# Turned scores in two products on operands laid out by transfers, a ring for x, and new orders and banks

## The chip, the cores and the metric

The kernel runs on one core of one Trainium2 chip. Five engines work side by side, each with its own instruction stream: TensorE (PE) multiplies matrices into eight PSUM banks, VectorE (DVE), ScalarE (ACT) and GpSimd (POOL) do elementwise work, and SyncE (SP) issues the transfers (DMA) between device memory and on-chip memory. They wait for each other through semaphores. The metric is the device time of one execution in microseconds.

## What is computed

A batch of 64 images with 256 positions and 320 channels passes two cross-attention layers, each with 20 heads of 16 channels and a context of 77 tokens of 512 channels.

```
layer 0:  q = x Wq^T,  k = text Wk^T,  v = text Wv^T          (77 text tokens)
          out = softmax(q k^T / 4) v  per head;  x = out Wo^T + bo + x
layer 1:  73 text tokens and 4 image tokens
          q = x W_q;  text_out = softmax(q k^T / 4) v;  probs_t = the same softmax
          qsem = l2norm(probs_t text);  sem = qsem . l2norm(image tokens)
          fused = q k_ip^T / 4 + 0.5 sem;  probs_ip = softmax(fused) * spatial_mask
          out = (text_out + probs_ip v_ip) W_out + b_out + x
```

## The kernel before

**Two stages.** `keys_and_values` multiplies the whole context with the key, value and image weights, in eight chunks of eight batches, and stores keys, values and the Gram matrix of the text (used for the norm of qsem) to device memory (`k_dram`, `v_dram`, `g_dram`). `attention` then runs over the 64 batches, both layers.

**Precision by parts.** Inputs are float32. A product that must be accurate is made from float16 parts: a high part and a low part, the rest. For q k^T three products are summed: high keys with high q, high keys with low q, low keys with high q.

**Layout.** 320 channels are three chunks of 128, the last one with its 64 channels doubled. A group of 32 partitions holds two heads of 16 channels. Keys are stored twice, once with zeros for the even head of a group and once with zeros for the odd one (`half_keys` with its `e`, scaled by `pscale`), so that a multiply over 32 partitions sees one head alone.

**Scores twice.** `scores` (L979) multiplies high parts only, with positions on the output partitions, and VectorE takes the negated maxima over the tokens (`maxima`, L1202). The maxima are turned by a transpose (`turn_max`) and copied to `mt`. `turned_scores` (L1009) makes the scores again with the tokens on the output partitions: three products, and a fourth that adds the maxima, for which a table of ones (`sel`) is the stationary operand. Four multiplies, one on each group of 32 rows, stand side by side. The exponential (`exponentials`, L1143) follows on ScalarE. In layer 1 ScalarE then halves it to float16 (`halves`), GpSimd takes the rest, TensorE multiplies with the Gram matrix (`gram_products`, L1053), VectorE weights the result (`weighted`, L1230), and `square_norms` sums it.

**What sets the order.** Every engine runs a cyclic list of steps, `ORDER` (L126). A step such as `1u2/3` means layer 1, gram product of unit 2, of the batch three behind the newest; `q` is the query projection, `s` scores, `m` turn of maxima, `t` turned scores, `a` attention sums, `n` norms, `i` and `p` the image tokens' scores and output, `o` the output projection, `y0` to `y19` the steps of the image softmax, `w` the weighting, `ql` the low part of q, `d` inverses, `g` and `at`/`al` the attended rows, `r` the residual. On SP, `k`, `v`, `x` load, `ds`, `sh`, `rw`, `rl` move denominators, move numerators, store and spread inverses. `USES` (L144) gives for each of the eight banks the cycle of its users; `Turns.wait` (L188) makes a step wait until the previous user of each of its banks has been read. Steps on one engine never overtake each other, and SP issues all transfers in the order of its list.

**Buffers.** x of layer 0 and of layer 1 have two buffers each, the residual with bias (`res`) and the output (`outt`) have two of their own, the spread inverses `rb` have one for each layer. The even head's numerators are moved to their partitions by four transfers (L894).

## Time and profile before

| | us |
|---|---|
| three timed runs | 2445.96, 2448.13, 2452.12 |
| median | 2448.13 |
| span of the profiled execution | 2447.7 |
| TensorE busy | 2259.4 (92%) |
| ScalarE busy | 1728.4 (71%) |
| VectorE busy | 1702.0 (70%) |
| GpSimd busy | 1592.2 (65%) |
| DMA queue q1, share of 16 engines | 44.7% |

The page gives no time of the profiled execution besides its span, so the time to compare with is 2447.7 us. Up to about 319 us the first stage runs, then the loop over batches. Busy time of TensorE is the time in which at least one multiply is in flight; a row that groups multiplies which run side by side adds their overlapping times only partly. A timeline row merges neighbours of one form; its first number is the start, the second the time to the end of the last. "PEclk" is the granted clock as a share of full speed.

### The profile page before, as it was taken

Reading aid. Unit: us, or ns where it says so; the run is one execution under the profiler, and the core shown is the slowest. Engines: PE = TensorE matmul, PEld = TensorE weight load, DVE = VectorE, ACT = ScalarE, POOL = GpSimd, SP = SyncE. Lnnn points to the kernel's source line nnn. Section 1 sums busy time; section 2 is a strip of 40 time slices with the busy share of each in tenths; the row PEclk is TensorE's granted clock in tenths of the full one; section 3 lists DMA queues with packets and bytes.
Section 4 is the critical chain, followed back from the end, with each engine's and each line's share of the span. In section 5 each row is a group of like instructions: output and inputs, shape, how many; then the busy total and the mean of one; then the engine's idle time right before and its main releaser. Section 6 shows DMA issues by size and latency. Waiting matters only on the chain.

```text
span 2447.7 us, 90636 instructions
## 1 busy us (share of the span) xinstructions
PE 2259.4 (92%) x35896; PEld 1464.0 (60%) x35896; DVE 1702.0 (70%) x2860; ACT 1728.4 (71%) x2604; POOL 1592.2 (65%) x1056
## 2 busy tenths in 40 slices
PE   8999958999999999999999999999999999999984
PEld 6777735655566665666556555666566655555642
DVE  5543425777777777777777777777777777777763
ACT  4332327778878777787787787877877787787861
POOL 4121135777777777777777776777777777777762
PEclk9999969999999999999999999999999999999996
DMA  9968622444444444444344444444444444444421
GB/s 275 281 209 235 194 89 70 117 115 117 118 114 114 118 115 116 118 115 117 111 118 119 115 114 114 113 118 115 115 118 118 114 113 115 114 119 116 119 80 56
DMA packets 338318, 310.92 MB, mean 127 GB/s; under 512 B 180224, under 2 KB 281856, under 8 KB 337920
## 3 DMA queue, kind: packets, MB, share of 16 engines
q1 hardware_dynamic: 337920, 305.36, 44.7%
q8 instruction: 281, 4.60, 0.8%
q14 instruction: 117, 0.96, 0.1%
HBM read 164.66 MB, written 105.98 MB: 111 GB/s over the span
## 4 chain that ended last, share of the span: by engine, by line
PE 46%; DVE 23%; ACT 7%; issue 5%; DMA 3%; SPq 2%; DVEq 0%; POOL 0%; ACTq 0%; POOLq 0%
PE psum L1065 12%; PE psum L966 10%; PE psum L1049 8%; PE psum L1028 7%; DVE q_low L1220 4%; ACT q_high L1136 4%; DVE mneg L1213 3%; PE psum L969 3%; ACT ef L1154 3%; DVE e L1235 3%; DVE sq L1254 2%; DVE outt L1313 2%; PE psum L1032 2%; PE psum L991 2%; DVE x1b L1313 1%
## 5 line engine op out<-in xcount | busy, mean ns | idle before, releaser
L1381 POOL TENSOR_TENSOR e<-ef,eh 73x1024 f32<-73x1024 f32 x320 | 681.1, 2129 | 300.4 <-ACT eh L1169 257.0
L1154 ACT ACTIVATE ef<-psum 73x1024 f32<-73x1024 f32 (+1 forms) x640 | 628.0, 1011 | 90.9 <-PE psum L1032 87.4
L1235 DVE TENSOR_TENSOR e<-psum,e 73x1024 f32<-73x1024 f32 x320 | 386.7, 1209 | 135.6 <-PE psum L1065 135.3
L1213 DVE TENSOR_REDUCE mneg<-psum 128x8 f16<-128x616 f32 (+3 forms) x512 | 446.9, 923 | 34.9 <-PE psum L991 34.1
L1065 PE MATMUL psum<-eh,gram 128*73 128x512 f16 x1280 | 340.9, 390 | 45.2 <-ACT ef L1154 16.0
L1049 PE MATMUL psum<-ef,values 128*32 128x256 f32 x5120 | 351.4, 389 | 7.7 <-DVE pip L1295 5.9
L1028 PE MATMUL psum<-q_high,keys 32*73 32x256 f16 (+2 forms) x6144 | 324.7, 258 | 34.0 <-DVE mneg L1213 21.6
L1169 ACT ACTIVATE eh<-ef 73x1024 f16<-73x1024 f32 x320 | 337.0, 1053 | 16.2 <-ACT ef L1154 0.4
L1220 DVE SCALAR_TENSOR_TENSOR q_low<-psum,q_high 128x640 f16<-128x640 f32 x128 | 105.5, 824 | 262.3 <-ACT q_high L1136 262.3
L1028 PEld LDWEIGHTS psum<-q_high,keys 32*73 32x73 f16 (+1 forms) x6144 | 186.9, 110 | 144.5 <-issue 68.7
L1162 ACT ACTIVATE ust<-psum 128x512 f32<-128x512 f32 x384 | 223.4, 594 | 67.1 <-PE psum L1049 60.5
L1348 POOL TENSOR_TENSOR al<-ust,ah 128x768 f16<-128x768 f32 x128 | 210.6, 1645 | 86.9 <-ACT ah L1192 86.6
L1343 POOL TENSOR_TENSOR ust<-ust,rb 128x768 f32<-128x768 f32 x128 | 231.8, 1811 | 17.9 <-DMA rb<-r_dram 17.8
L1065 PEld LDWEIGHTS psum<-eh,gram 128*73 128x73 f16 x1280 | 121.9, 115 | 173.0 <-ACT ef L1154 47.0
L1049 PEld LDWEIGHTS psum<-ef,values 128*32 128x32 f32 x5120 | 128.9, 109 | 136.3 <-issue 30.4
L966 PE MATMUL psum<-ah,wo 128*128 128x256 f16 x1280 | 194.7, 275 | 13.2 <-POOL al L1348 13.2
L1032 PE MATMUL psum<-mt,sel 32*73 32x256 f16 (+3 forms) x3072 | 205.2, 251 | 0.0
L1028 PE MATMUL psum<-q_low,keys 32*73 32x256 f16 (+3 forms) x3072 | 205.2, 251 | 0.0
L1077 PE MATMUL psum<-e,pick 128*32 128x256 f32 x2560 | 165.8, 386 | 2.6 <-DVE e L1235 2.6
L966 PE MATMUL psum<-xh,wq 128*128 128x256 f16 x1024 | 155.8, 275 | 5.7 <-PEq L230 4.1
L1192 ACT ACTIVATE ah<-ust 128x768 f16<-128x768 f32 x128 | 107.5, 840 | 66.1 <-POOL ust L1343 56.2
L966 PEld LDWEIGHTS psum<-ah,wo 128*128 128x128 f16 x1280 | 119.2, 98 | 45.3 <-DVE e L1235 17.4
(180 smaller groups left out, 4530.3 us busy)
## 6 DMA issues: line engine op xcount, KB each, us to landing
rb<-r_dram SPq DMA_DIRECT2D x128, 384.0 KB, 4.1
keys<-k_dram SPq DMA_DIRECT2D x128, 231.0 KB, 3.6
values<-v_dram SPq DMA_DIRECT2D x128, 192.5 KB
ust<-ust SPq DMA_DIRECT2D x512, 48.0 KB, 2.5
v_dram<-vst SPq DMA_DIRECT2D x64, 320.0 KB
out<-outt SPq DMA_DIRECT2D x64, 320.0 KB, 2.2
k_dram<-kst SPq DMA_DIRECT2D x32, 616.0 KB, 4.8
x<-in_x SPq DMA_DIRECT2D x32, 384.0 KB, 3.7
```

The source lines that it names most:

```text
L966: mm = pe.matmul(o[:, c * S:(c + 1) * S], a, data[:, k, :], **at_ends)
L1028: pe.matmul(o, keys(l, low, c)[rows, e, 0:n], q[rows, cols], start=(low == 0 and q is qh[l]), stop=False)
L1032: mm = pe.matmul(o, sel[rows, k, 0:n], mt[l][rows, lead:lead + many], start=False, stop=True)
L1049: mm = pe.matmul(row(l, f"a{c}")[j * SLOT:(j + 1) * SLOT, r * S:(r + 1) * S], va[l][:, h, :], e, start=True, stop=True)
L1065: mm = pe.matmul(banks(l, f"u{k}", 2)[0:n, r, :], gm[:, b.parity(), half, :], e, start=(half == 0), stop=(half == 1))
L1154: act.activation(ef[l][0:m, unit_heads(n), :].rearrange("t h s -> t (h s)"), src, ACT.Exp, scale=SM).then_inc(s_exp[l], 1)
L1162: act.activation(ust[l][:, b.parity(), :, c, :], src, ACT.Copy).then_inc(s_u[l], 1)
L1169: act.activation(eh[0:m, unit_heads(k), :], ef[1][0:m, unit_heads(k), :], ACT.Copy, scale=0.5)\
L1213: dve.tensor_reduce(dst, o, AX_X, ALU.max, negate=True).then_inc(s_max[l], 1)
L1235: dve.tensor_tensor(rest, banks(l, f"u{k}", 2)[0:m, :, :], rest, ALU.mult).then_inc(s_wr, 1)
L1343: pool.tensor_tensor(at(l, b), at(l, b), rb[l][:], ALU.mult).then_inc(s_at[l], 1)
L1381: pool.tensor_tensor(e2[0:m, k, :, :], ef[1][0:m, unit_heads(k), :], eh[0:m, unit_heads(k), :], ALU.subtract).then_inc(s_e2, 1)
```

## The change

- `turned_scores` has two products instead of four. The heads' channels are interleaved, so that in a group of 32 partitions even rows belong to one head and odd rows to the other. For one head, `tq` holds on the rows of that head's partner copies of its own q rows: on every pair of rows the same source row. The first product multiplies it with `paired_keys` (high keys on one row of a pair, low keys on the other), the second multiplies `marked_keys` (high keys on one row, ones at marked places on the other) with the low part of q and the maxima. Transfers build all this: `load_key_tiles` issues three for a set of keys, `turn_queries` (`tq`) two, `place_maxima` (`tm`) two.
- In the first stage keys are copied once, in high and low part, and stored in halves of their former size, with smaller rows.
- x lives in a ring of six buffers through both layers; bias, layer output and final output are written in place. `res` and `outt` are gone. `rb` is one buffer for both layers.
- Numerators are moved by one transfer instead of four, inverses stored once instead of twice and spread by two transfers.
- `ORDER` and `USES` are new; waits for banks come from the whole order, and a step that uses two banks can wait for the second one later (`only`).

```diff
-DEN, SEM4 = D, D + 1
+DEN = 1
+KC = CW * T
+QW = PW
+TW = QW + CW * S
+RING = 6
...
 ORDER = {
     "pe": """
-        1u2/3 1a1/3 0t1/1 1q/2 0t2/1 0a0/1 1s0/2 0a1/1 1s1/2 0a2/1 1a2/3 1i/2 1u3/3 1m/2 1u4/3 1t0/2 0q/0
-        1n0/3 1n1/3 1p/4 0s0/0 1n2/3 1n3/3 1n4/3 0s1/0 1t1/2 1a0/2 1u0/2 1t2/2 1u1/2 1o/4 0m/0 0o/1 0t0/0""",
+        0m/1 1u0/3 0o/2 1u1/3 0t0/1 1a1/3 1u2/3 0t1/1 1q/2 0t2/1 0a0/1 0a1/1 1s0/2 0a2/1 1n0/3 1a2/3 1s1/2 0q/0 1u3/3
+        1m/2 1u4/3 1n1/3 1p/4 1n2/3 1n3/3 1n4/3 1i/2 1t0/2 0s0/0 0s1/0 1t1/2 1o/4 1y/3 1t2/2 1a0/2""",
     "act": """
-        1a1/3 1f/4 0t2/1 0t3/1 1q/2 0t4/1 1h4/3 0a0/1 0a1/1 0a2/1 1a2/3 1i/2 1m/2 0r/0 1t0/2 1h0/2 0q/0
-        1t1/2 1h1/2 1n/3 1g/4 1t2/2 1t3/2 1a0/2 0g/1 1t4/2 1h2/2 0m/0 1r/2 1h3/2 0t0/0 0t1/0""",
+        1t4/3 1h1/3 0m/1 1h2/3 1a0/3 1h3/3 0t0/1 0t1/1 1a1/3 1f/4 0t2/1 0t3/1 1q/2 0t4/1 0a0/1 0a1/1 0a2/1 1h4/3 1a2/3
+        0r/0 1r/2 1m/2 0q/0 1g/4 1n/3 1i/2 1t0/2 1t1/2 1h0/2 1t2/2 1t3/2 0g/1""",
     "dve": """
-        1y10/4 1y11/4 0o/2 1y12/4 1y13/4 1y14/4 1w2/3 1y15/4 1y16/4 1y17/4 1y18/4 1y19/4 1ql/2 1s0/2 1s1/2
-        1s2/2 1s3/2 1w3/3 0d/1 1w4/3 0ql/0 1p/4 0s0/0 0s1/0 0s2/0 1d/3 0s3/0 1w0/2 1w1/2 1y0/3 1y1/3 1y2/3
-        1y3/3 1o/4 1y4/3 1y5/3 1y6/3 1y7/3 1y8/3 1y9/3""",
+        1y0/4 1y1/4 1y2/4 1y3/4 1y4/4 1y5/4 1w0/3 1y6/4 1y7/4 1y8/4 1y9/4 1y10/4 0o/2 1y11/4 1w1/3 1y12/4 1y13/4
+        1y14/4 1y15/4 1w2/3 1y16/4 1y17/4 1y18/4 1y19/4 1ql/2 1s0/2 1s1/2 1s2/2 1s3/2 0d/1 1w3/3 1w4/3 1p/4 0ql/0
+        0s0/0 0s1/0 0s2/0 0s3/0 1d/3 1o/4""",
     "pool": """
-        1xh/2 1xl/2 1b3/3 1b4/3 0xh/0 1vb/4 0xl/0 1kb/1 1c/2 1at/4 1b0/2 1b1/2 1al/4 0at/1 0al/1 1b2/2""",
+        0al/2 1b1/3 1b2/3 1xh/2 1xl/2 1b3/3 1at/4 0xh/0 0xl/0 1kb/2 1b4/3 1c/2 1vb/4 1al/4 0at/1 1b0/2""",
     "sp": """
-        1ss/3 1sl/3 1rl/4 1sh/4 0x/0 1vi/4 1ps/4 0ds/1 1v/2 1pl/4 1ds/3 0k/0 0rw/1 0sh/1 0rl/1 1g/2 1c/1
-        0v/0 1ns/3 1rw/3 1nl/3 1k/1 1d/3 1st/4""",
+        0x/0 1rw/4 1vi/4 0tm/1 0v/1 1rl/4 1c/2 1st/5 1sh/4 1k/2 1sl/3 1ps/4 0k/0 1tq/2 1pl/4 0ds/1 1v/2 0rw/1 1tm/2
+        0rl/1 1ds/3 0sh/1 1ns/3 1d/3 0tq/0 1nl/3 1g/1 1ss/2""",
...
 USES = [
-    "0t3/1 0a0/1 0a2/1 1u3/3 0q/0 0s0/0 0s2/0 1u1/2 0m/0 0t1/0",
-    "0t3/1 0t4/1 1s1/2 1u3/3 0q/0 0s0/0 0s2/0 1a0/2 1u1/2 0t1/0",
-    "1a1/3 0t4/1 1s1/2 1i/2 1u4/3 1n/3 1t2/2 1u0/2 1o/4",
-    "0t2/1 0t4/1 1s3/2 1u4/3 1p/4 1t2/2 1u0/2 1o/4 0t0/0",
-    "0t2/1 0t4/1 1s3/2 1t0/2 1p/4 0s3/0 1t4/2 0t0/0",
-    "1u2/3 1q/2 1s0/2 1s2/2 1m/2 1t0/2 1p/4 0s3/0 1t4/2 0o/1",
-    "1u2/3 1q/2 1s0/2 1s2/2 1t1/2 0s1/0 1t3/2 1t4/2 0o/1",
-    "0a1/1 1a2/3 1t1/2 0s1/0 1t3/2 1t4/2 1y/3",
+    "1u1 1u2 0t4 1n 0s0 0s3 1t4",
+    "1u1 1u2 0t4 1s1 0q 0s0 0s3 1t4",
+    "1u0 0t0 0t3 0t4 1s1 0q 0s1 1t3 1t4",
+    "1u0 0t0 0t3 0t4 1s0 1s3 1u3 1p 1i 0s1 1t3 1t4",
+    "1a1 1q 1s0 1s3 1u3 1p 1t1 1t2 1a0",
+    "0o 0t1 0t2 1q 0a2 1s2 1m 1p 1t1 1t2",
+    "0m 0o 0t1 0t2 0a0 1s2 1u4 1t0 0s2 1o",
+    "0a1 1a2 1u4 1t0 0s2 1o 1y",
...
+def load_key_tiles(sp, ka, ks, src, loaded):
+
+    both_parts = src.rearrange("a x (r f) n -> (a r) x (f n)", f=2)
+    sp.dma_start(ka[:].rearrange("p f n -> p (f n)"), both_parts).then_inc(loaded, 16)
+    for e in (0, 1):
+        high = src[:, 0, 1 - e:P:2, :].rearrange("a r n -> (a r) n")
+        sp.dma_start(ks[1 - e:P:2, e, :, :], high.unsqueeze(1).to_broadcast([HALF, 2, KC])).then_inc(loaded, 16)
+
+
+KLOADS = 3
...
+                dst = [k_dram[l][bass.DynSlice(batch, CB), :, :, :].rearrange("b x p n -> x p b n") for l in both]
+                for l in both:
+                    results_of("k", l, 1)
+                    for x in (0, 1):
+                        keys = kst[l][:, x, :, :, :].rearrange("p b c t -> p b (c t)")
+                        sp.dma_start(dst[l][x, :, :, 0:2 * T], keys).then_inc(s_kstored, 16)
+                results_of("kt", 0, 1)
+                for l in both:
+                    for x in (0, 1):
                         for copy in (0, 1):
-                            tail = ktail[l * HALF:(l + 1) * HALF, half, :, :, :, :].rearrange("p b h e t -> p b (h e t)")
-                            sp.dma_start(dst[l][copy * HALF:(copy + 1) * HALF, :, 8 * T:], tail)\
-                              .then_inc(s_kstored[half], 16)
+                            sp.dma_start(dst[l][x, copy * HALF:(copy + 1) * HALF, :, 2 * T:],
+                                         ktail[l * HALF:(l + 1) * HALF, x, :, :]).then_inc(s_kstored, 16)
...
-                        for e in (0, 1):
-                            ins = act.activation(half_keys(kind, l, c, half, 0, e), by_batch(psum[:, r, 0:HT], T), ACT.Copy,
-                                                 scale=pscale[:, e:e + 1])
-                        ins.then_inc(s_khigh, 1)
+                        act.activation(half_keys(kind, l, c, half, 0), by_batch(psum[:, r, 0:HT], T), ACT.Copy,
+                                       scale=1 / WS).then_inc(s_khigh, 1)
...
+        xr = [early.xin] + [sb(f"x_ring{n}", [P, CW, S]) for n in range(1, RING)]
         xh = [early.xh, sb("xh1", [P, CW, S], F16)]
         xl = [early.xl, sb("xl1", [P, CW, S], F16)]
-        res = [sb(f"res{l}", [P, 2, (CW * S, PW)[l]]) for l in both]
-        qh = [sb(f"q_high{l}", [P, PW], F16) for l in both]
-        ql = [sb(f"q_low{l}", [P, PW], F16) for l in both]
-        ke = [early.ke, sb("keys1", [P, 2 * CW * 2 * T], F16)]
+        qq = [sb(f"q_parts{l}", [P, 2, QW], F16) for l in both]
+        qh, ql = [[qq[l][:, n, :] for l in both] for n in (0, 1)]
+        tq = [sb(f"turned{l}", [P, 2, TW], F16) for l in both]
+        ka = [early.ka, sb("keys1", [P, 2, KC], F16)]
+        ks = early.ks
...
+        def plain_keys(l, c):
+            return ks[l][:, :, 0, c * T:(c + 1) * T]
+
+        def paired_keys(l, e, c):
+            return ka[l][:, 1 - e, c * T:(c + 1) * T]
+
+        def marked_keys(l, e, c):
+            return ks[l][:, e, 1, c * T:(c + 1) * T]
...
+            def turn_queries(l, b, n):
+
+                b.reached(sp, f_t[l], CW, 0)
+                b.reached(sp, s_ql[l], 1, 1)
+                for e in (0, 1):
+                    rows = qq[l][1 - e:P:2, :, :].rearrange("p h n -> p (h n)")
+                    sp.dma_start(tq[l][:, e, 0:2 * QW], rows.unsqueeze(1).to_broadcast([HALF, 2, 2 * QW]))\
+                      .then_inc(s_tq[l], 16)
+
+            def place_maxima(l, b, n):
+
+                b.reached(sp, s_tq[l], 32, 32)
+                b.reached(sp, s_mt[l], 1, 1)
+                for e in (0, 1):
+                    dst = tq[l][e:P:2, e, QW:].rearrange("p (c s) -> p c s", c=CW)
+                    sp.dma_start(dst, mt[l][e:P:2, :].unsqueeze(1).to_broadcast([HALF, CW, S])).then_inc(s_tm[l], 16)
...
-                for j in range(NJ):
-                    sp.dma_start(ust[l][j * SLOT + D:(j + 1) * SLOT, b.parity(), 0, :, :],
-                                 ust[l][j * SLOT:j * SLOT + D, b.parity(), 1, :, :]).then_inc(s_num[l], 16)
+                sp.dma_start(ust[l][1:P:2, b.parity(), 0, :, :], ust[l][0:P:2, b.parity(), 1, :, :]).then_inc(s_num[l], 16)
 
             def store_inverses(l, b, n):
                 b.reached(sp, s_rd[l], 1, 1)
-                for copy in (0, 1):
-                    dst = r_dram[l][b.parity()][:, copy, :].rearrange("h (q i) -> h q i", i=QS)
-                    sp.dma_start(dst, rd[l][:, b.parity(), :]).then_inc(s_rw[l], 16)
+                dst = r_dram[l][b.parity()].rearrange("j r (q i) -> (j r) q i", i=QS)
+                sp.dma_start(dst, rd[l][:, b.parity(), :]).then_inc(s_rw[l], 16)
 
             def spread_inverses(l, b, n):
                 b.reached(sp, s_at[l], 1, 0)
-                b.reached(sp, s_rw[l], 32, 32)
-                src = r_dram[l][b.parity()].rearrange("h k n -> (h k) n").unsqueeze(1).to_broadcast([2 * HC, D // 2, CW * S])
-                sp.dma_start(rb[l][:].rearrange("p c s -> p (c s)"), src).then_inc(s_rb[l], 16)
+                before = spread_before(l, b)
+                if before is not None:
+                    sp.wait_ge(s_at[before[0]], before[1] + 1)
+                b.reached(sp, s_rw[l], 16, 16)
+                for r in (0, 1):
+                    src = r_dram[l][b.parity()][:, r, :].unsqueeze(1).to_broadcast([NJ, D, CW * S])
+                    sp.dma_start(rb[r:P:2, :, :].rearrange("p c s -> p (c s)"), src).then_inc(s_rb[l], 16)
...
-                    b.reached(pe, s_ql[l], 1, 1)
-                    b.reached(pe, s_mt[l], 1, 1)
+                    b.reached(pe, s_tm[l], 32, 32)
                 for e in range(2):
                     if c < 2:
                         tiles = [(slice(j * SLOT, (j + 1) * SLOT),
                                   banks(l, uses[j // 2], 2)[0:n, j % 2, e * S:(e + 1) * S]) for j in range(NJ)]
-                        cols, many = slice(c * S, (c + 1) * S), S
+                        cols = slice(c * S, (c + 1) * S)
                     else:
                         tiles = [(slice(j * SLOT, (j + 1) * SLOT), banks(l, "t4", 4)[0:n, j, e * TS:(e + 1) * TS])
                                  for j in range(NJ)]
-                        cols, many = slice(2 * S, PW), TS
-                    for low, q in ((0, qh[l]), (0, ql[l]), (1, qh[l])):
-                        for rows, o in tiles:
-                            pe.matmul(o, keys(l, low, c)[rows, e, 0:n], q[rows, cols], start=(low == 0 and q is qh[l]),
-                                      stop=False)
+                        cols = slice(2 * S, PW)
                     for rows, o in tiles:
-                        k, lead = (2 * c + e, 0) if c < 2 else (2 * c, e * many)
-                        mm = pe.matmul(o, sel[rows, k, 0:n], mt[l][rows, lead:lead + many], start=False, stop=True)
+                        pe.matmul(o, paired_keys(l, e, c)[rows, 0:n], tq[l][rows, e, cols], start=True, stop=False)
+                    for rows, o in tiles:
+                        mm = pe.matmul(o, marked_keys(l, e, c)[rows, 0:n], tq[l][rows, e, QW:2 * QW][:, cols], start=False,
+                                       stop=True)
...
                 b.reached(pe, s_eh, UNITS, k + 1)
                 for r in range(2):
+                    if r:
+                        wait_free(pe, l, b, f"u{k}", only=1)
...
             def residual(l, b, n):
-                b.reached(act, (s_x, s_xo[0])[l], (16, 1)[l], (16, 1)[l])
-                b.reached(act, s_xo[l], 1, -1)
+                b.reached(act, s_xl[l], 1, 1)
+                data = x_of(b)
                 for c in range(CW if l == 0 else 2):
-                    ins = act.activation(res[l][:, b.parity(), c * S:(c + 1) * S], xin[l][b.parity()][:, c, :], ACT.Identity,
-                                         bias=bias_sb[l][:, c:c + 1])
+                    ins = act.activation(data[:, c, :], data[:, c, :], ACT.Identity, bias=bias_sb[l][:, c:c + 1])
...
             def output(l, b, n):
                 b.reached(dve, s_rs[l], 1, 1)
-                if l == 0:
-                    b.reached(dve, s_xl[1], 1, -1)
-                    b.reached(dve, s_rs[1], 1, -1)
-                else:
-                    b.reached(dve, s_store, 16, -16)
                 b.reached(dve, f_o[l], 1, 1)
-                dst, n = (xin[1][b.parity()][:].rearrange("p c s -> p (c s)"), CW * S) if l == 0 else (outt[:, b.parity(), :], PW)
-                dve.scalar_tensor_tensor(dst, row(l, "o", 2)[:, 0:n], 1 / WS, res[l][:, b.parity(), :], ALU.mult,
+                data, n = x_of(b)[:].rearrange("p c s -> p (c s)"), (CW * S, PW)[l]
+                dve.scalar_tensor_tensor(data[:, 0:n], row(l, "o", 2)[:, 0:n], 1 / WS, data[:, 0:n], ALU.mult,
```

## Rows read from the trace of the kernel before

**Rows 1.** busy by stage: start:end, length, PE, PEld, DVE, ACT, POOL, PEclk, DMA, GB/s
```profile
180.00:240.00 60.00, 60.00 (x642) 47.35 (x641) 21.96 (x52) 17.31 (x41) 9.15 (x2) 1.00 0.85 242
...
330.00:360.00 30.00, 12.67 (x195) 8.01 (x196) 5.42 (x7) 9.94 (x15) 11.05 (x7) 0.61 0.22 59
...
420.00:1100.00 680.00, 646.56 (x11019) 408.30 (x11021) 519.41 (x865) 543.36 (x796) 502.16 (x342) 1.00 0.42 115
...
1254.92:1286.54 31.62, 30.18 (x519) 19.01 (x515) 24.25 (x40) 25.29 (x38) 23.52 (x17) 1.00 0.43 116
```

**Rows 2.** page, costliest groups: line, engine, operation, tiles, count, busy us, mean ns
```profile
L1235 DVE TENSOR_TENSOR e<-psum,e 73x1024 f32<-73x1024 f32 x320 | 386.7, 1209 | 135.6 <-PE psum L1065 135.3
...
L1028 PE MATMUL psum<-q_high,keys 32*73 32x256 f16 (+2 forms) x6144 | 324.7, 258 | 34.0 <-DVE mneg L1213 21.6
...
L1032 PE MATMUL psum<-mt,sel 32*73 32x256 f16 (+3 forms) x3072 | 205.2, 251 | 0.0
L1028 PE MATMUL psum<-q_low,keys 32*73 32x256 f16 (+3 forms) x3072 | 205.2, 251 | 0.0
```

**Rows 3.** timeline of TensorE, turned scores: start, time to the end, line, forms
```profile
1275.35 0.25 PE L1028 MATMUL psum<-q_high,keys 32*73 32x128 f16 x4
...
1282.07 0.31 PE L1028 MATMUL psum<-q_high,keys 32*77 32x256 f16 x4
...
1282.86 0.28 PE L1032 MATMUL psum<-mt,sel 32*77 32x256 f16 x4
```

**Rows 4.** timeline of TensorE, starts of long steps and of what follows them
```profile
1265.31 0.61 PE L966 MATMUL psum<-xh,wq 128*128 128x256 f16 x4
...
1267.73 1.07 PE L1077 MATMUL psum<-e,pick 128*32 128x256 f32 x16
...
1275.93 1.06 PE L1065 MATMUL psum<-eh,gram 128*73 128x512 f16 x4
1276.82 0.60 PE L966 MATMUL psum<-ah,wo 128*128 128x256 f16 x4
...
1279.23 0.29 PE L1005 MATMUL psum<-ident,mneg 128*128 128x128 f16 x2
```

**Rows 5.** timeline of VectorE, ScalarE and TensorE behind an output and turned scores
```profile
1282.53 0.96 DVE L1313 SCALAR_TENSOR_TENSOR x1b<-psum,res 128x768 f32<-128x768 f32 x1
...
1283.34 1.91 ACT L1154 ACTIVATE ef<-psum 77x1024 f32<-77x1024 f32 x2
...
1283.55 1.06 PE L1065 MATMUL psum<-eh,gram 128*73 128x512 f16 x4 [0.41 <-DVE x1b L1313]
```

**Rows 6.** timeline of ScalarE, copies behind the norms
```profile
1271.51 0.38 ACT L1175 ACTIVATE nst<-psum 128x256 f32<-128x256 f32 x1 [0.81 <-PE psum L1077]
1271.79 0.84 ACT L1192 ACTIVATE ah<-ust 128x768 f16<-128x768 f32 x1
```

**Rows 7.** timeline of TensorE and VectorE, two score steps and the maxima
```profile
1259.25 0.31 PE L991 MATMUL psum<-keys,q_high 32*128 32x146 f16 x8 [0.26 <-DVE q_low L1220]
...
1260.51 0.31 PE L991 MATMUL psum<-keys,q_high 32*128 32x146 f16 x8
...
1259.68 3.39 DVE L1213 TENSOR_REDUCE mneg<-psum 128x8 f16<-128x584 f32 x4 [0.49 <-PE psum L991]
```

**Rows 8.** transfers, 1000 to 1640 us: packets, MB, share; issues, KB, us to landing
```profile
q1 hardware_dynamic: 82241, 72.38, 41.3%
...
rb<-r_dram SPq DMA_DIRECT2D x41, 384.0 KB, 4.2
...
ust<-ust SPq DMA_DIRECT2D x164, 48.0 KB, 2.5
```

**Rows 9.** timeline of SyncE, issues of transfers in one period
```profile
1265.40 1.42 SPq L901 DMA_DIRECT2D r_dram<-rd  x2
...
1269.86 0.56 SPq L907 DMA_DIRECT2D rb<-r_dram  x1
```

**Rows 10.** transfers, 0 to 300 us: packets, MB, share of 16 engines
```profile
q1 hardware_dynamic: 72750, 71.98, 81.2%
```

297 lines of the change are left out of this document (151 added, 146 removed).

## The prediction

> **What bounds the kernel now.** Read the stage table first, then the costliest lines, then a period's timeline. In the projection stage TensorE is busy without a gap (60.00 of 60.00 us) at a granted clock of 1.00; in the attention loop it is busy 646.56 of 680 us, ScalarE 543, VectorE 519, GpSimd 502 [rows 1]. One period, from one layer-1 query projection to the next, takes 31.62 us; over many, 31.7. TensorE ends the period, but the other three have 24 to 25 us of work in it. A change that shortens TensorE by more than a few us meets them, and all four feed each other through the banks.
>
> The turned scores look like the largest item: 12,288 multiplies on L1028 and L1032, whose groups' busy times sum to 735 us [rows 2], 11.5 us a period. That sum is a trap. Four multiplies on four row groups run together, and the next four follow 0.11 us later while the first are still in flight: eight such groups start between 1282.07 and 1282.86, so a whole step takes 0.88 us and not eight times 0.28; the short step, from 1275.35 to the next step at 1275.93, takes half of it, 0.47, and a gap [rows 3, 4]. A period has four long steps and two short ones: 4.5 us of TensorE's time, not 11.5.
>
> **The change on TensorE.** Each step goes from eight groups to four: a long one 0.88 to 0.45 us, a short one 0.47 to 0.25. Saved: 4 x 0.43 + 2 x 0.22 = 2.2 us a period, 64 x 2.2 = 138 us, if nothing else ends there. By steps, from the start of one to the start of the next, what stays: five gram steps of 0.89 (1275.93 to 1276.82), two query projections of 2.42, the output projections of 2.41 and, with the turn of the maxima in front, 2.84 (1279.23 to 1282.07) [rows 3, 4], attention sums, norms, scores and the small ones together about 10 us; with the new turned scores 27.3 us. Before: 29.4, so 2.3 us of each 31.7 were waits.
>
> **What the new order waits for.** I walked the new orders and bank lists through one period, time 0 at the layer-0 turn of the maxima, with durations of the rows, and looked for each step at the last reader of its banks.
> - 1u0 follows the exponential of 1t4 in the same bank: start 0.45 instead of 0.1.
> - 0o ends at 4.1. 0t1 has its banks, so VectorE's output add must be through; from the output's last issue to TensorE's next start that took 1.48 us (1282.07 to 1283.55, the add 0.96) [rows 3, 5]: 0t0 at 5.55, a wait of 0.55.
> - 0t1 takes the banks of 0t0's two exponentials, 1.91 us for the pair [rows 5]: 8.45, a wait of 0.5. Then 1q, 0t2 and two sums, 1s0 at 13.7, 0q from 15.75, 1u3 until 19.1.
> - VectorE weights 1u3 and 1u4 (1.21 us each [rows 2]) and adds the image part (0.96, as the add of the same size in rows 5): 22.6. ScalarE then copies 0.84, 0.38 and about 0.37 [rows 6]: 24.25. 0s0 needs the bank of the last: 24.4.
> - 0s1 comes straight behind 0s0, and its second use has 0s0's banks. Start of scores to start of the maxima 0.43, and to the next scores 1.26 [rows 7]. Before, three norm steps filled this; now nothing does: 0s1 at 25.65, a wait of 1.0.
> - 1t1 waits for two exponentials (26.55, a wait of 0.6), 1o for the third maximum of layer 0 (27.5, 0.4). 1o 2.41, 1t2 0.4, 1a0 0.9: the next turn at 31.25.
> Waits with two small ones (1t0 and 0s0, 0.45 together): 3.9 us. The period is 27.3 + 3.9 = 31.2, I take 31.25: of 2.2 us saved, 1.6 go back into waits, most of them in the 4 us around 0s0, where ScalarE's own chain would end only some 0.6 us earlier. So 64 x 0.45 = 29 us are gained.
>
> **The transfers.** Added per layer and batch: two of 320 KB that lay out the interleaved rows (256 packets of 2560 B) and two that place the maxima (384 packets of 512 B); key loads go from 1 to 3 (128 packets to 384, same bytes). Away: three of four numerator moves and one inverse store. Per period (640 us hold 20.2) the bytes go from 3.6 to 5.3 MB, the packets from 4070 to 5670 [rows 8]. A packet now takes 51 ns (0.413 x 16 x 640 us over 82,241) [rows 8]; at that, 290 engine-us of 16 x 31.25 = 500, 58%; by bytes 310, 62%. Not a bound as a sum.
>
> A wait is added in front of the turned scores: maxima copied, then two issues, then landing. No row shows this transfer. The nearest small one, 48 KB, lands in 2.5 us, the 384 KB one in 4.2 [rows 8]; an issue takes 0.6 to 0.7 [rows 9]. From below 0.7 + 2.5 = 3.2 us, from above 1.4 + 4.2 = 5.6. The order leaves 3.8 us on layer 0 (mt 1.75, 0t0 5.55) and 3.3 on layer 1 (20.35 to 23.65). I take 3.2, the row nearest in size: just hidden. At the upper end both are late and a period would be up to 4.1 us longer. Queued behind the waiting placement on SP are the values, the inverses' spread and the layer-1 stores; GpSimd's multiply by the inverses waits for these, with 2 us to spare in my walk. The query layout is issued about 5 us ahead of its use and hidden.
>
> SP itself: 35 issues a period become 41. At 0.56 to 0.71 us each [rows 9] that is 23 to 29 us of 31.25, with landings to wait for in between (inverses, norms, probabilities).
>
> The single buffer for the inverses couples the layers; its reader is done 10 us before the next load. The ring for x and the residual in place take two buffers and no work away. Nothing on these, from -0.1 to +0.2 us a period: the waits they replace (load of x, output store) end no step in the rows.
>
> **Stage one.** Keys are copied once instead of twice on ScalarE and VectorE. TensorE fills that stage alone [rows 1], so this is worth nothing. Key stores halve in bytes but double in packets (4096 to 8192 a chunk, of 308 and 154 B). Mean cost of a packet now: 0.812 x 16 x 300 us / 72,750 = 54 ns [rows 10]. Per chunk of 36 us the DMA time changes by -7 us (by bytes) to +14 (by packets). With 29 us used (81%) it becomes 22 to 43 us. I take about +3, since in the loop 60% of the packets are under 512 B and the mean is still 51 ns [rows 8]: hidden behind TensorE, 0 us.
>
> **Filling and draining.** In the first and last periods one batch's chain sets the time (TensorE 12.67 of 30 us busy, clock 0.61 [rows 1]). The placement of the maxima stands in it bare: about 2.5 us more for each layer at one end, +5 us (bounds 0 to +20).
>
> **Sum.** The profiled execution's span is 2447.7, the median of the runs 2448.1; they agree within 0.5, and I go from the latter. 2448 - 29 + 5 = 2424.
>
> **Rivals.**
> A, TensorE alone decides: its waits stay at 2.3 us a period although the work shrinks. 2448 - 138 + 5 = 2315. For it: TensorE is the busiest by 5 us. Against: the bank reuse at 0s1, 0t0 and 0t1 is forced by the list. Half of it (waits 3.1) gives 2366.
> B, slower: the placement of maxima is late. SP comes to it late behind the x load, the inverse store and the wait for norms (in my walk it gets there about when the maxima do), or the transfer queues behind 655 KB of query rows. It decides from 0.45 us a period on; with 0.5 us on each layer, 1.0 in all, the period is 32.25 and the time 2448 + 35 + 5 = 2488. For it: SP has 2 to 8 us left, the slack on layer 1 is 0.1. Against: DMA is idle 40% of the time.
> C, slower in stage one: small packets cost as much as large ones, DMA needs 43 us for 36 of TensorE, 7 us x 7 chunks = +49: 2473. Against: the loop's 51 ns. The Trainium skill (DMA: Bandwidth & Descriptors, Specifications) says that transfers below 512 B fall short of the line rate since a read-modify-write is done; by that rule both new store sizes pay, and C is what it would give. The rows do not separate packet sizes, so it is not settled by them.
> D, the clock: TensorE's busy share falls from 0.95 to 0.90. [...] Left at 2%.
>
> **Chances.** My forecast (2395 to 2445) 0.45; A or its half 0.20; B 0.21; C 0.08; the rest (D, a walk wrong by more, other causes) 0.06. A walk of this kind errs by some 0.6 us a period, 38 us. The range 2350 to 2478 leaves out A in full and the bad end of B. About 0.3% (7 us) can be told from no change: faster 0.59, within 0.14, slower 0.27.
>
> **What would show it.** Steps of turned scores of 0.45 us. A gap of about 1 us on TensorE between the first and second score steps of layer 0, released by the maxima; gaps of 0.5 before 0t0 (output add) and 0t1 (exponentials). If the first is absent, A gains. TensorE waiting for a transfer ahead of the turned scores is B. Stage one ending later than 319 us, with DMA above 95%, is C. A loop period outside 30.6 to 31.9 us would make the forecast wrong.

## The result, and the profile after

The changed kernel takes 2704.44 us, median of four runs (2696.22 to 2715.94); the kernel before took 2449.61 us on the same chip (2445.96 to 2452.12). The ratio is 1.1046, 95% interval 1.1015 to 1.1077: 255 us slower, where 2424 us was forecast and the range ended at 2478. The profiled execution took 2707.64 us, its span is 2705.8 us.

The stage table of the changed kernel, with the columns of [rows 1]; the first two windows lie in the projection stage, the third where the first batch fills the loop:

```profile
120.00:180.00 60.00, 60.00 (x558) 46.65 (x556) 12.31 (x31) 8.54 (x22) 15.16 (x4) 1.00 1.18 134
180.00:240.00 60.00, 60.00 (x643) 47.40 (x641) 15.36 (x41) 12.55 (x34) 12.29 (x3) 1.00 0.94 202
330.00:360.00 30.00, 9.13 (x114) 5.47 (x118) 8.65 (x6) 7.27 (x10) 17.32 (x10) 0.56 0.36 125
420.00:1100.00 680.00, 567.50 (x7952) 343.53 (x7950) 467.64 (x754) 466.41 (x702) 444.53 (x304) 0.94 0.49 147
```

Against [rows 1] every engine does less in the loop: TensorE 567.50 of 680 us instead of 646.56, ScalarE 466 instead of 543. No engine has become the bound. What rises is the transfers' share, 0.42 to 0.49, which still looks far from full. The granted clock falls from 1.00 to 0.94. A period, from one store of the image probabilities (L978) to the next, runs from 1209.92 to 1246.38 us: 36.5 us instead of 31.62; 18 periods in 640 us make 35.6 on average against 31.7. The two profiled spans differ by 258 us. 18 of these lie in the projection stage, which ends at 337.6 instead of 319.7 us; the other 240 are the longer periods.

The chain of waits of the page names who sets the end, first by engine and then by line, each with its share of the span:

```profile
DMA 29%; PE 19%; SPq 14%; issue 9%; POOL 9%; DVE 4%; ACT 3%; POOLq 0%; ACTq 0%; DVEq 0%
DMA rb<-r_dram 13%; PE psum L1014 10%; DMA den<-ust 5%; DMA n_dram<-nst 5%; POOL ust L1391 4%; SPq L888 3%; DMA r_dram<-rd 2%; PE psum L1113 2%; SPq L953 2%; POOL al L1396 2%; ACT ef L1207 2%; PE psum L1075 2%; SPq L245 2%; SPq L879 2%; PE psum L1017 2%
```

The first is a transfer, the spread of the inverses. The same chain inside one period (start, length, what):

```profile
1214.58 4.37 DMA den<-ust
...
1219.04 0.56 DVE rd L1281
1219.61 0.31 SPq L943
...
1220.02 0.66 SPq L888
1220.72 0.64 SPq L888
...
1221.47 0.57 SPq L953
1222.08 6.61 DMA rb<-r_dram
1228.73 0.82 issue
1229.58 1.82 POOL ust L1391
...
1233.44 1.64 POOL al L1396
...
1235.22 4.33 PE psum L1014 x24
```

Denominators land, VectorE inverts them, the inverses are stored, two placements of maxima are issued in between, then the spread takes 6.61 us to land. GpSimd waits for it, and TensorE for GpSimd. The output projection at the end takes 4.33 us for 24 multiplies, since the granted clock is 0.50 in its first 3 us. Four windows of the changed kernel show that: an output at full clock; a gap of TensorE, behind which come one gram step at full clock and another wait of 0.85 us; the slow output; and what follows.

```profile
1227.40:1230.10 2.70, 2.68 (x48) 2.22 (x48) 1.62 (x3) 1.74 (x2) 0.52 (x1) 1.00 0.50 171
1231.60:1233.20 1.60, 0.00 (x0) 0.00 (x0) 0.00 (x0) 1.60 (x3) 1.60 (x1) 1.00 0.33 96
1235.20:1238.20 3.00, 2.98 (x15) 2.13 (x16) 2.79 (x9) 1.65 (x3) 3.00 (x2) 0.50 0.55 151
1239.00:1242.00 3.00, 2.70 (x41) 1.51 (x39) 2.35 (x4) 0.55 (x1) 1.36 (x3) 1.00 0.69 202
```

A granted clock of 0.50 is 1.2 GHz. So a transfer that is late by 4 us can cost more than 4 us: from its start to the next step the slow output takes 4.16 us, the one at full clock 2.42. This is no exception. Between 420 and 2300 us, in some 53 periods, the clock records of the changed kernel have 50 stretches at 0.50, 188 us together; those of the kernel before have one. The landings, from 1000 to 1640 us (issues, KB each, median us to landing), beside [rows 8]:

```profile
q1 hardware_dynamic: 102930, 94.13, 49.2%
...
turned<-q_parts SPq DMA_DIRECT2D x72, 320.0 KB, 3.9
rb<-r_dram SPq DMA_DIRECT2D x72, 192.0 KB
...
turned<-mt SPq DMA_DIRECT2D x72, 96.0 KB, 2.1
...
ust<-ust SPq DMA_DIRECT2D x36, 192.0 KB, 6.3
```

Packets and bytes are as forecast (5720 and 5.2 MB a period; 5670 and 5.3). The new placement of maxima lands in 2.1 us, sooner than the forecast took. The move of the numerators (2.5 us before, in four pieces of 48 KB) needs 6.3. Why, is seen in the first batch, where little else is on the way. SyncE issues the spread at 367.20 us, the move of the numerators at 368.38, query rows at 369.02 and a load of x at 370.92. By the packet records, the packets of 3072 bytes, which are those of the spread and of the move, keep 4.1 engines busy in each of the four microseconds from 371 to 375. Then the other twelve engines are through with all their work. Two windows of what is left, changed kernel:

```profile
375.00:376.00 1.00, 0.00 (x0) 0.00 (x0) 0.00 (x0) 0.00 (x0) 0.00 (x0) 0.50 0.24 93
376.00:377.00 1.00, 0.00 (x0) 0.00 (x0) 0.00 (x0) 0.00 (x0) 0.94 (x1) 0.50 0.25 100
```

A share of 0.25 over 16 engines is four engines working and twelve idle. What the four still carry is, after the last packets of 3072 bytes, mostly not the spread: it is 64 of the 256 packets of the query rows and then, until 378.5 us, 96 of the 384 packets of x, a quarter of each, which had stood behind it. In the kernel before, a window in the middle of the spread (issued at 351.29 us, landed 3.65 us later):

```profile
353.00:354.00 1.00, 0.37 (x2) 0.14 (x2) 0.00 (x0) 0.00 (x0) 0.00 (x0) 0.50 1.02 306
```

Here packets of 3072 bytes keep 15.2 engines busy. In the packet records of the loop they are four at once for 47% of the time in which any is in flight; before, all numbers up to 16 occur. The same bytes queue on a quarter of the engines, and each other transfer that has packets for those four stands behind them. The Trainium skill (DMA: Bandwidth & Descriptors, "Why a DMA increments its semaphore by 16 and not by 1") has the rule: the number of engines is the largest up to 16 that divides the slowest dimension of both sides. By that rule the old source with 16 blocks in its slowest dimension uses 16 engines and the new one with four (one for each row group, NJ) uses four; the windows above agree.

### The profile page after: what moved, and what is told of

Its sections match the earlier page's. It is cut to its first block, busy times and chain, and to the rows that moved or that the text cites. A ratio compares the mean times of both kernels' runs of the same rounds, so it can differ in the third digit from the quotient of the medians.

```text
span 2705.8 us, 78624 instructions
## 1 busy us (share of the span) xinstructions
PE 2214.7 (82%) x29752; PEld 1392.6 (51%) x29752; DVE 1691.3 (63%) x2780; ACT 1635.9 (60%) x2523; POOL 1588.5 (59%) x1056
## 4 chain that ended last, share of the span: by engine, by line
DMA 29%; PE 19%; SPq 14%; issue 9%; POOL 9%; DVE 4%; ACT 3%; POOLq 0%; ACTq 0%; DVEq 0%
DMA rb<-r_dram 13%; PE psum L1014 10%; DMA den<-ust 5%; DMA n_dram<-nst 5%; POOL ust L1391 4%; SPq L888 3%; DMA r_dram<-rd 2%; PE psum L1113 2%; SPq L953 2%; POOL al L1396 2%; ACT ef L1207 2%; PE psum L1075 2%; SPq L245 2%; SPq L879 2%; PE psum L1017 2%
## 5 line engine op out<-in xcount | busy, mean ns | idle before, releaser
L1095 PE MATMUL psum<-ef,values 128*32 128x256 f32 x5120 | 344.5, 387 | 1.3 <-DVE pip L1348 0.7
L1014 PE MATMUL psum<-ah,wo 128*128 128x256 f16 x1280 | 234.7, 315 | 75.6 <-POOL al L1396 62.8
L1075 PE MATMUL psum<-turned,keys 32*73 32x256 f16 (+3 forms) x3072 | 191.4, 274 | 105.0 <-issue 34.8
L1014 PEld LDWEIGHTS psum<-ah,wo 128*128 128x128 f16 x1280 | 132.9, 111 | 152.5 <-issue 92.3
L1075 PEld LDWEIGHTS psum<-turned,keys 32*73 32x73 f16 (+1 forms) x3072 | 97.9, 113 | 196.5 <-issue 102.0
L1095 PEld LDWEIGHTS psum<-ef,values 128*32 128x32 f32 x5120 | 142.3, 110 | 101.0 <-issue 16.0
L1281 DVE RECIPROCAL rd<-den 96x64 f32<-96x64 f32 x128 | 70.2, 548 | 198.3 <-DMA den<-ust 197.9
L1077 PE MATMUL psum<-turned,own_keys 32*73 32x256 f16 (+3 forms) x3072 | 184.7, 262 | 0.0
L1386 POOL TENSOR_TENSOR xl<-x_ring,xh 128x768 f16<-128x768 f32 x106 | 174.1, 1642 | 15.7 <-POOL xh L1379 0.6
L1125 PE MATMUL psum<-e,pick 128*32 128x256 f32 x2560 | 180.0, 390 | 1.5 <-DVE e L1288 1.4
```

The lines of the kernel that those rows point to most:

```text
L1014: mm = pe.matmul(o[:, c * S:(c + 1) * S], a, data[:, k, :], **at_ends)
L1075: pe.matmul(o, paired_keys(l, e, c)[rows, 0:n], tq[l][rows, e, cols], start=True, stop=False)
L1095: mm = pe.matmul(row(l, f"a{c}")[j * SLOT:(j + 1) * SLOT, r * S:(r + 1) * S], va[l][:, h, :], e, start=True, stop=True)
```

## Experiments

Three theories stood. **Theory 1**: the spread on four engines is the loss. **Theory 2**: the volume of the new query rows is. **Theory 3**: SyncE's queue, 41 issues a period instead of 35, is. Beside them, how much TensorE's saving and the key rows of stage one are worth by themselves. Each ratio, with its 95% interval, is to the kernel before in runs shared with it, whose median was 2448 to 2455 us in the different sets. Where two edited kernels of different sets are compared, the difference of their medians is good to some 10 us only.

**The spread on 16 engines, by two issues more for each layer.**

```diff
-                for r in (0, 1):
-                    src = r_dram[l][b.parity()][:, r, :].unsqueeze(1).to_broadcast([NJ, D, CW * S])
-                    sp.dma_start(rb[r:P:2, :, :]..., src).then_inc(s_rb[l], 16)
+                for j in range(NJ):
+                    src = r_dram[l][b.parity()][j:j + 1, :, :].to_broadcast([D, 2, CW * S])
+                    sp.dma_start(rb[j * SLOT:(j + 1) * SLOT, :, :]..., src).then_inc(s_rb[l], 16)
```

> The changed kernel (2704 us, 35.9 us a period) with the spread of the inverses issued as four transfers, one for each group of 32 partitions, so that its slowest dimension is 16 and no longer 4; everything else as changed. Theory 1 (the spread runs on four of the 16 engines and everything behind it on these four is late): the transfer lands in about 4 us instead of 6.6, the numerators behind it too, a period falls by 2 to 3.5 us to 32.5 to 34, the time to 2490 to 2580. Theory 2 (the 655 KB of query rows hold up what is behind them): little changes, above 2650, since these bytes stay. Theory 3 (SP's queue of issues is the bound): four more issues a period at 0.6 us, so 2704 or up to 150 us slower.

2662.77 us, ratio 1.0851 (1.0803 to 1.0898). The landings are as theory 1 says:

```profile
rb<-r_dram SPq DMA_DIRECT2D x148, 96.0 KB, 2.6
...
ust<-ust SPq DMA_DIRECT2D x37, 192.0 KB, 2.2
```

but only 42 us came back, far less than theory 1 said. SyncE's issues are now 43% of the chain of waits, where they were 14%; some of one period:

```profile
1215.57 0.65 SPq L888
1216.26 0.63 SPq L888
1216.99 0.61 SPq L953
1217.64 0.59 SPq L953
1218.28 0.99 SPq L953
1219.31 0.59 SPq L953
1220.00 0.60 SPq L922
```

Two things changed at once here, the engines and the issues (41 to 45). They had to be told apart.

**Short query rows.** After the first batch only a quarter of each query row is laid out (a part of the operand stays that of the first batch).

```diff
-                    rows = qq[l][1 - e:P:2, :, :].rearrange("p h n -> p (h n)")
-                    sp.dma_start(tq[l][:, e, 0:2 * QW], rows.unsqueeze(1).to_broadcast([HALF, 2, 2 * QW]))
+                    many = 2 * QW if first(b) else QW // 2
+                    rows = qq[l][1 - e:P:2, :, :].rearrange("p h n -> p (h n)")[:, 0:many]
+                    sp.dma_start(tq[l][:, e, 0:many], rows.unsqueeze(1).to_broadcast([HALF, 2, many]))
```

> The changed kernel, but after the first batch the query layout transfers move only a quarter of each row (640 B instead of 2560 B); the rest of the operand keeps the first batch's values. Same number of packets and issues. Theory 1: a gain below 60 us, since the spread keeps its four engines busy for 6 us. Theory 2: the landings of spread and numerators shorten by 1.5 to 2 us, a period by 2 us or more, 2570 or less. Theory 3: no change within 20 us.

2717.27 us, ratio 1.1073 (1.1012 to 1.1133), as slow as the changed kernel. Theory 2 falls for this kernel; the run with four tiny transfers, below, asks the same once more with the spread on 16 engines.

**Two products in the old kernel.** The low products of the turned scores are left out, nothing else.

```diff
-                    for low, q in ((0, qh[l]), (0, ql[l]), (1, qh[l])):
+                    for low, q in ((0, qh[l]),):
```

> The kernel before, with the two products of the low parts left out of the turned scores (high keys with high q, and the maxima, remain), so two products of four; orders, banks and transfers as before. It prices the TensorE term alone. My forecast's saving was 2.2 us a period with old waits kept: 2449 - 138 = 2311. If the old order gives a part back in waits on VectorE and ScalarE, 2330 to 2400. If TensorE is not what ends the period, 2440 or more.

2435.14 us, ratio 0.9908 (0.988 to 0.9936). This is what the change is for, by itself:

```profile
420.00:1100.00 680.00, 612.56 (x9030) 362.96 (x9026) 529.55 (x871) 543.91 (x804) 506.81 (x346) 1.00 0.42 116
```

TensorE's busy time falls by 34 us in the 680, 1.6 a period, but the time by 20 us only (2454.63 for the kernel before in the same set), 0.3 a period. Rival A (TensorE alone decides, 138 us) is dead on the old kernel's own order.

**Long key rows in stage one.** The stores write one run a partition for eight batches, 2464 and 1232 bytes instead of 308 and 154 (the keys' arrangement in DRAM is then not the one that stage two expects).

```diff
-                        sp.dma_start(dst[l][x, :, :, 0:2 * T], keys).then_inc(s_kstored, 16)
+                        sp.dma_start(dst[l][:, x * CB * KC:x * CB * KC + 2 * CB * T],
+                                     keys.rearrange("p b n -> p (b n)")).then_inc(s_kstored, 16)
...
```

> The changed kernel, but the first stage stores the same key bytes as rows of 2464 and 1232 B instead of 308 and 154 B (the keys land in another arrangement than the second stage reads, so the scores differ). Small rows as the cause of the longer first stage: it ends at about 319 us as before, not 337, the DMA share there falls from 1.0 to about 0.65, and the time falls by 18 us to about 2686. If the stage is longer for another reason (one counter for both halves of the keys, later stores): the end stays near 337.

2680.28 us, ratio 1.0922 (1.0879 to 1.0965), 24 us less. The first 300 us of the changed kernel:

```profile
q1 hardware_dynamic: 97748, 55.03, 103.2%
```

and with long rows:

```profile
q1 hardware_dynamic: 48912, 57.33, 61.9%
```

Half the packets, more bytes, and 61.9% instead of 103.2%: packets of 154 and 308 bytes made the stage wait for its transfers. It ended at 337.6 us in the changed kernel, 319.7 before and about 319 here.

**Four issues fewer, on 16 engines.** The second of the two placed key copies and the second of the two query-row copies of each layer are made for the first batch only. That is the changed kernel's count, 41.

```diff
-                for e in (0, 1):
+                for e in (0, 1) if first(b) else (0,):
                     rows = qq[l][1 - e:P:2, :, :].rearrange("p h n -> p (h n)")
```

> The kernel with the inverses spread on 16 engines, and four of SyncE's 45 issues a period left out after the first batch (the second of the two placed key copies and the second of the two query-row copies, of each layer; what they would write stays that of the first batch; TensorE's, ScalarE's and VectorE's work is the same). Theory 3 (SyncE's queue has become the bound: in the chain of the profile with 16 engines nearly each piece of a period is one of its issues, 0.6 us each): 4 x 0.62 = 2.5 us a period, 66 periods, 2500 us, and 2490 to 2570 with what is given back. Rival (the issues are in the chain only because the profile puts waits down to them, and the bound is a landing or an engine): under 0.5 us a period, 2630 to 2665.

2496.72 us, ratio 1.0202 (1.0185 to 1.0219). At the same 41 issues as the changed kernel this is 208 us faster. But the two differ in more than the spread's engines: four transfers are left out, and four issues spread the inverses where two did. The table further down separates them.

**Another order of the 45 issues.**

```diff
-        ... 1ps/4 0k/0 1tq/2 1pl/4 0ds/1 1v/2 0rw/1 1tm/2
-        0rl/1 1ds/3 ...
+        ... 1ps/4 0k/0 1tq/2 0ds/1 1pl/4 1v/2 1tm/2 0rw/1
+        1ds/3 0rl/1 ...
```

> The kernel with the inverses spread on 16 engines and the same 45 issues in another order: layer 0's denominators are sent before layer 1's probabilities are fetched, and the placement of layer 1's maxima and layer 1's denominators stand in the two gaps in which SyncE waited (4.4 us until the inverses of layer 0 are there, then until they are stored). Theory 3 (SyncE's queue is the bound, issues and unfilled waits together): three issues fill some 2 of the 4.4 us of wait, 66 x 2 = 130 us, 2530 us, range 2500 to 2600. Rival (the queue follows the engines, and its waits are where slack shows up): the wait only moves, 2640 to 2690.

2621.01 us, ratio 1.0729 (1.0689 to 1.077): 42 us, neither the 130 nor the nothing. The wait for the denominators' inverses is gone from SyncE (64.1 us of 640 before the edit, none after). In its place SyncE waits 41.7 us for copied maxima and 17.1 for the landing of the stored inverses, and this landing, 2.4 and 4.2 us in one period, stands in the chain.

**The old kernel with its spread on four engines.** Same bytes, same issues, but four blocks in the source's slowest dimension (only four rows of inverses are spread). The expectation says 40 blocks for the kernel before; its source has 2 x HC = 16.

```diff
-                src = r_dram[l][b.parity()].rearrange("h k n -> (h k) n").unsqueeze(1).to_broadcast([2 * HC, D // 2, CW * S])
+                src = r_dram[l][b.parity()][0:NJ, 0, :].unsqueeze(1).to_broadcast([NJ, P // NJ, CW * S])
```

> The kernel before with one edit: the inverses' source has four blocks in its slowest dimension instead of 40, as in the changed kernel (of the inverses only four rows are spread; bytes and issues are the same). Theory 1 (the spread on four engines lands 2 to 4 us later, and its landing stands in the chain of each layer): landing from 4.2 to 7 us or more; two spreads a period, one of them in the chain, 66 x 1 to 2 us: 2510 to 2590. Rival (the landing is late only in the changed kernel, with its single buffer and its full queue; the old order of work has the slack): 2450 to 2470.

2692.72 us, ratio 1.1023 (1.0987 to 1.1059): one line brings the old kernel to the changed one's time, above my upper 2590. What GpSimd's multiply by the inverses waits for, 1000 to 1640 us (us, times):

```profile
  DMA rb<-r_dram: 33.6, 18
```

where the trace of before shows no wait. And in the chain, once a period, a load of values:

```profile
1199.55 2.68 DMA values<-v_dram
...
1234.27 2.92 DMA values<-v_dram
```

The reader is not the only one that is late. I had priced the spread's own landing; what it also does is hold up whatever is queued behind it: x lands in 6.3 us instead of 3.7, and GpSimd waits 16.7 us of 640 for it (3.5 before); the image probabilities are stored in 5.1 us instead of 3.1. The values in the chain are issued 9.5 us behind the last spread, so they are not shown to be held up by it.

**Order and long rows together.**

```diff
-        ... 1tq/2 1pl/4 0ds/1 1v/2 0rw/1 1tm/2 0rl/1 1ds/3 ...
+        ... 1tq/2 0ds/1 1pl/4 1v/2 1tm/2 0rw/1 1ds/3 0rl/1 ...
-                        sp.dma_start(dst[l][x, :, :, 0:2 * T], keys)
+                        sp.dma_start(dst[l][:, x * CB * KC:x * CB * KC + 2 * CB * T], ...)
```

> The kernel with the inverses spread on 16 engines and the other issue order, and the keys stored in rows of 2464 and 1232 bytes in stage one (the keys' arrangement in DRAM isn't that which the loads of stage two expect; counts, sizes and issues of stage two are the same). The stages' costs add: the time of the other-order kernel less 24 us (what long rows were worth alone), so 2505 by theory 3, 2640 by its rival. If the two shared a cause they would not add.

2603.79 us, ratio 1.0645 (1.0623 to 1.0666), 17 us under the other order alone: the stages' costs nearly add.

**Seven issues given by ScalarE.**

```diff
-program("sp", {"x": load_x, "k": load_keys, "v": load_values, "g": load_gram, "c": load_c4, "vi": load_vip, ..., "st": store})
+program("sp", {"k": load_keys, ...})
+program("act", {..., **transfers(act)})        # x, v, g, c, vi, st
```

> The kernel with the inverses spread on 16 engines, and seven of the 45 issues a period (x, both layers' values, gram, c4, image values and the output's store) given by ScalarE instead of SyncE: the same transfers, 38 issues on SyncE. Theory 3 (SyncE's queue is the bound of that kernel): 7 x 0.62 = 4.3 us a period off the queue; four issues fewer were worth 166 us in all, and the next bounds are near, so 2450 to 2510. ScalarE is busy 0.75 of the time there, and an issue may hold it: if it costs ScalarE 0.6 us each as it does SyncE, 4.2 us of a period of 33, 2500 to 2580. Rival (the gain of the run with four issues fewer came from the transfers left out, not from the queue): 2640 to 2690.

2786.48 us, ratio 1.137 (1.1335 to 1.1406), the slowest of all, outside both expectations. The denominators' inverses came later still (SyncE waited 92.0 us of 640 for them, 64.1 before the edit) and the granted clock fell to 0.92 in the loop. ScalarE's additional load cannot be blamed alone, since I also had to choose places in ScalarE's order; which of the two it was is open. It does not count against a bound by SyncE, nor for it.

**Four issues fewer, on four engines.** The edit of the 2497 us run, but with the spread as the change has it.

```diff
-                for e in (0, 1):
+                for e in (0, 1) if first(b) else (0,):
```

> The changed kernel, its inverses spread on four engines as it stands, with the same four issues a period left out after the first batch as in the run of 2497 us (37 issues). If the spread on four engines is a bound of its own (the old kernel with such a spread took 2693 us), fewer issues are worth little here: 2640 to 2700. If its cost was only that it lengthened SyncE's waits, the issues that are saved are worth here what they were worth there, 166 us: 2520 to 2560.

2686.99 us, ratio 1.0958 (1.0928 to 1.0989). The table is now complete:

```
issues a period     37      41      45
4 engines         2687    2704
16 engines                2497    2663
```

On four engines four issues are worth 17 us, on 16 engines 166. The other way round, with the other transfers equal, 16 engines for four are worth 42 us (2704 to 2663) while all transfers are made, and 190 us (2687 to 2497) without those four. Each bound hides the other; only both together give the 208 us.

**Six issues more in the old kernel**, the keys loaded by four transfers of 32 partitions.

```diff
-                sp.dma_start(ke[l][:], src).then_inc(s_ke[l], 16)
+                for j in range(NJ):
+                    rows = slice(j * SLOT, (j + 1) * SLOT)
+                    sp.dma_start(ke[l][rows, :], src[rows, :]).then_inc(s_ke[l], 16)
```

> The kernel before, its keys loaded by four transfers of 32 partitions instead of one, for each layer: six issues a period more on SyncE, 41 as in the changed kernel, same bytes and engines. SyncE waited some 9 us of 31.7 in a period there; six issues are 3.7 us and fit if those waits can be used: 2445 to 2480 by theory 3. If a queue of 41 issues is already the bound whatever its waits, 2520 to 2600.

2580.59 us, ratio 1.0516 (1.0471 to 1.0562): 128 us where I expected at most 30. SyncE's timeline in a period, old kernel with the split (start, length):

```profile
1262.57 0.58 SPq L879 DMA_DIRECT2D den<-ust  x1
1263.19 2.08 SPq L845 DMA_DIRECT2D keys<-k_dram  x4
1265.33 1.43 SPq L903 DMA_DIRECT2D r_dram<-rd  x2
```

and the kernel before:

```profile
1264.24 0.59 SPq L877 DMA_DIRECT2D den<-ust  x1
1264.87 0.47 SPq L843 DMA_DIRECT2D keys<-k_dram  x1
```

The keys stand right in front of the store of layer 0's inverses. (The move at 1264.24 is that of layer 1's denominators; layer 0's had gone out at 1262.20.) VectorE had these inverses ready at 1265.08 in the kernel before, and the store came 0.3 us later ([rows 9]); in the edited kernel they were ready at 1263.38, and the store came 1.95 us later. These 1.6 us a period are most of the 2.0 that 128 us over 64 make. SyncE's free 9 us lie elsewhere in the period and don't help. GpSimd waits 18.6 us of 640 for the spread, for which the trace of before shows no wait.

**Fewer issues in the old kernel**: gram, c4 and image values loaded for eight batches at once, 32.6 issues instead of 35.

```diff
+                if b.index() % G:
+                    return
-                src = g_dram[bass.DynSlice(b.index(), 1), :, :].rearrange("a t n -> (a t) n")
+                src = g_dram[bass.DynSlice(b.index(), G), :, :].rearrange("a t n -> t a n")
```

> The kernel before with gram, c4 and image values loaded for eight batches at a time instead of for each: 0.6 issues a period for these instead of 3, so 32.6 on SyncE instead of 35, same bytes. Theory 3 carried to the old kernel (an issue on SyncE has a price there at every count, 128 us / 6 = 21 us each by the run with six more): 2.4 x 21 = 50 us, 2400, range 2395 to 2435. Rival (the price starts where SyncE's free time ends, and at 35 issues it has some: it waited 9 us of 31.7 a period): 2440 to 2455.

2454.13 us, ratio 1.0006 (0.9992 to 1.0019), nothing. In the trace of before SyncE waits anyway shortly behind them: 1.2 us behind gram and c4, 3.6 behind the image values. Here an issue has no price of its own; its place decides.

**The same grouping in the other-order kernel, and in the four-issues-fewer kernel with long rows.**

```diff
-        gm = sb("gram", [P, 2, 2, TXT[1]], F16)
+        gm = sb("gram", [P, 2 * G, 2, TXT[1]], F16)
-                b.reached(sp, f_u, UNITS, -UNITS)
+                b.reached(sp, f_u, UNITS, -UNITS * G)
```

> The kernel with the inverses spread on 16 engines in the other issue order (2621 us), with the same three loads grouped by eight batches: 42.6 issues a period instead of 45. By the price that four fewer issues had at this count (166 us, 41 each): 2.4 x 41 = 98 us, 2520, range 2500 to 2560. Rival (those four were worth more because the transfers left out carried 1.3 KB rows to all partitions and their landings stood in the chain; an issue alone is worth 0.6 us or less a period): 2570 to 2600.

> The changed kernel with the inverses on 16 engines, the four issues a period left out after the first batch (2497 us), the three loads grouped (38.6 issues on SyncE) and the keys stored in long rows in stage one (the keys' arrangement in DRAM isn't what stage two expects). If what is left of the loss is issues and small rows only: 2497 - 24 - 50 to 98 = 2375 to 2425, under the kernel before. Rival (another cost of the change stands in the 49 us, and issues are no longer the bound): 2450 to 2475.

2643.16 us, ratio 1.0785 (1.0769 to 1.08), 22 us above the other order alone; and 2481.52 us, ratio 1.0135 (1.0106 to 1.0163), 15 us below its base, about what the long rows give. Both missed: grouping gives nothing. The 22 us in the one order are hardly clear of the spread of the runs (2610 to 2636 without grouping, 2631 to 2646 with it), and I found no reason for them.

**The four issues kept, their bytes taken away**: 64 bytes a row after the first batch.

```diff
-                    sp.dma_start(tq[l][:, e, 0:2 * QW], ...)
+                    n = 2 * QW if first(b) or e == 0 else 32
+                    sp.dma_start(tq[l][:, e, 0:n], ...)
```

> The kernel with the inverses spread on 16 engines, all 45 issues a period kept, but the second placed key copy and the second query-row copy of each layer carry 64 bytes a row after the first batch (0.9 MB a period less; what they would write stays that of the first batch). If the 166 us of the run without these four were the price of SyncE's issues: 2640 to 2665. If they were that of their bytes and of their late landing: 2495 to 2520. Between: both, in that share.

2667.78 us, ratio 1.0888 (1.0841 to 1.0935): all of the 166 us stay (the bytes fell by 0.76 MB a period, not 0.9). They are the price of four transfers in these places, and none of it of their bytes. The edit keeps the number of packets, but those of 64 bytes take 11 ns each, and the share of the DMA engines fell from 50.3% to 44.8%. It also keeps the waits for their landings, but no wait of an engine in the trace is put down to one. What is left is their issues.

**Eight engines in the old kernel**, with one store of the inverses and with two.

```diff
-                for copy in (0, 1):
+                for copy in (0,):                 # in the first of the two only
...
-                src = r_dram[l][b.parity()].rearrange("h k n -> (h k) n").unsqueeze(1).to_broadcast([2 * HC, D // 2, CW * S])
+                src = r_dram[l][b.parity()][:, 0, :].unsqueeze(1).to_broadcast([HC, D, CW * S])
```

> The kernel before with the inverses stored once instead of twice and spread from eight blocks instead of 16: 33 issues a period, the reference's output. Two effects: on eight engines the spread's packets take twice the time that they take on 16, so the landing goes from 4.2 to about 5 us (on four, alone, it made 245 us); and one issue of SyncE and one small landing less stand ahead of each spread, 0.6 us of the chain from denominators to attended. If few engines cost in proportion to their queue: 80 us more less 20 to 40, 2490 to 2510. If eight engines still hide it: 2420 to 2450.

> The kernel before, its inverses stored twice as they are, spread from eight blocks: eight engines, same issues. If few engines cost in proportion to their queue (245 us at four): some 80 us, 2510 to 2550. If the old kernel hides a landing of up to about 5 us: 2448 to 2465.

2465.76 us, ratio 1.0067 (1.0045 to 1.0089), and 2504.65 us, ratio 1.0212 (1.0174 to 1.025). Both lie between their two expectations. 16, 8 and 4 engines are 0, 54 and 245 us: not in proportion, each halving costs more. One issue of the store fewer for each layer gives back 39 us, again an issue in front of the spread. No kernel that does the whole computation beats the kernel before.

## Why the prediction was wrong

**The step that failed** is in "The transfers": it compared the transfers as a sum over 16 engines, "58%; by bytes 310, 62%. Not a bound as a sum", and had no term for a later landing of the inverses' spread, 4.2 us in its rows. Of the edit to the spread it priced only the shared buffer ("Nothing on these"). The diff shows the source going from 16 blocks to NJ = 4, and that makes four engines of 16. The landing measured 6.61 us in the chain, and the numerators' move behind it 6.3 us, where the same 192 KB take 2.2 with the spread on 16 engines. GpSimd's multiply, given 2 us to spare in the walk, waits 103.6 us in 35 multiplies for its data. In the kernel before, this one edit makes a loss of 245 us by itself. In the changed kernel it is not the whole: putting it right alone gives back 42 us, since the next bound, SyncE's queue, lies close behind; with four transfers less as well it is 208. The costs share the same slack and don't add (245 + 128 + 24 is more than the 255 seen).

**SyncE's queue** was costed as "23 to 29 us of 31.25" and let pass, as it is less than the period. The runs show that the sum is the wrong question. Six issues more in the old kernel were worth 128 us, three of them in front of a store of the inverses, and 2.4 issues a period nothing elsewhere. Behind the spread this is the next bound, and the second half of what failed: 166 us for four issues, once 16 engines carry it. Rival B named SyncE as late, but for the placement of the maxima, which was on time: in 640 us TensorE waited 3.7 us in two places for it. Its 2488 us was right in sign alone.

**TensorE** came out as worked out. A long step of turned scores and the start of the next, then a short one:

```profile
1226.45 0.31 PE L1075 MATMUL psum<-turned,keys 32*73 32x256 f16 x4 [0.32 <-DVE mneg L1266]
1226.56 0.31 PE L1077 MATMUL psum<-turned,own_keys 32*73 32x256 f16 x4
1226.67 0.31 PE L1075 MATMUL psum<-turned,keys 32*73 32x256 f16 x4
1226.78 0.31 PE L1077 MATMUL psum<-turned,own_keys 32*73 32x256 f16 x4
...
1243.80 0.28 PE L1077 MATMUL psum<-turned,own_keys 32*77 32x256 f16 x4
1244.01 0.61 PE L1014 MATMUL psum<-xh,wq 128*128 128x256 f16 x4
...
1246.42 0.25 PE L1075 MATMUL psum<-turned,keys 32*77 32x128 f16 x4
```

Four groups of four 0.11 us apart, 0.45 with the last; 0.25 for the short one, as said. The gap between the two score steps of layer 0 was to be 1.0 us, released by the maxima:

```profile
1224.36 0.32 PE L1040 MATMUL psum<-own_keys,q_parts 32*128 32x154 f16 x8 [0.57 <-ACT nst L1228]
1225.74 0.32 PE L1040 MATMUL psum<-own_keys,q_parts 32*128 32x154 f16 x8 [1.06 <-DVE mneg L1266]
```

It is 1.06. The period was to lie between 30.6 and 31.9 us, and by its own words the forecast is wrong with the 35.6 measured. That the work taken from TensorE mostly turns into waits was right: in the old kernel without the low products 20 us are left of 138. But the 29 us rested on a walk in which nothing else was late, and a walk of TensorE's orders cannot see a queue on four transfer engines.

**Stage one** was costed at 0, and rival C at 49 us with a chance of 0.08. C's signs came (the stage ends at 337.6 us, the share in two windows of it is 1.18 and 0.94), but long rows took back 24 us, about half of its price. "60% of the packets are under 512 B and the mean is still 51 ns" was no bound from above. In the packet records of that loop most of the small packets are of 256 bytes and take 17 ns, and those of 3072 bytes take 178; the mean of both says nothing about the stores of stage one, whose packets of 154 and 308 bytes took 41 and 46 ns. The mean in stage one was 51 ns again, but at a third more packets than before in the same time, and that filled the engines (103.2%). The measured 24 us are halfway between the 0 forecast and the 49 of its upper bound (43 us for 36 of TensorE). The Trainium skill (DMA: Bandwidth & Descriptors, Specifications) says that transfers below 512 bytes fall short of the line rate. The experiment with long rows agrees in direction.

**The clock** was rival D, left at 2% and without a term. It fell behind gaps in which TensorE waited for late data, and may be no small part of the loss: 0.50 in 50 stretches of the loop, and 1.7 us more for an output in the chain. Once a period, that would be up to 1.7 of the 3.9 us by which the period grew, an estimate from the two outputs above; no run separates it.

**What stays open.** With 16 engines and 41 issues the kernel is still 49 us behind; 15 to 24 of these are the key rows. The rest would be SyncE's six issues more than before, by the experiment on the old kernel, but no run took exactly these away. In that kernel the granted clock is still 0.50 in 33 stretches of the loop. The new orders, the new bank lists and the ring for x were in every edit of the changed kernel and were never run by themselves, so a share of theirs isn't excluded. Nor is it known why ScalarE as a second issuer costs time.

## What to carry to other kernels

For each transfer that a change rewrites, read the slowest dimension of both sides before its bytes: a mean share of 0.49 over 16 engines can hide stretches with four full engines and twelve empty ones, and everything with packets for those four is late. Count the issues that stand on the queue between the two ends of a chain (here: denominators moved, inverses stored, inverses spread), not the issues of a period. And if taking work from the busiest engine is the aim, take it away alone first: here that showed 20 us of 138, which could be known before any layout was rebuilt.

## What the runs showed of the hardware that was not expected

- A spread of 384 KB from 16, 8 and 4 blocks made 0, 54 and 245 us in the same kernel. With eight blocks eight packets of 3072 bytes are in flight most often (29% of the time), with four blocks four (49%).
- A transfer issue holds SyncE for some 0.6 us whatever its bytes: the median of the query rows' issues was 0.61 us with all at 2560 bytes a row and 0.60 with half of them at 64, and the time 2663 and 2668 us.
- Small packets are hardly cheaper than middle ones in stage one's stores: in its packet records those of 154 and 308 bytes took 41 and 46 ns on average, in the kernel before those of 616 and 1232 bytes 43 and 57. In the loop it is otherwise: 17 ns for 256 bytes, 54 for 1024.
- The granted clock was still 1.00 in a 1.60 us window without any multiply and in the gram step behind it, and 0.50 in the output behind the next wait, of 0.85 us.
